# Zero rows up to 128 for every matmul that contracts over 40 or 16 rows, in a graph layer with a mixture of experts

## The chip, the cores and the metric

The kernel runs on one core of a Trainium2 chip. Its time is the device time of one execution in microseconds (us); a kernel's time is the median of its runs. TensorE is called PE below, its weight loads PEld, VectorE DVE, ScalarE ACT, GpSimd POOL, and the engine that issues most loads SP.

## The reference

There are 10000 tokens and 10000 items of width 128. A dense 10000 x 10000 adjacency matrix (400 MB in float32) is multiplied with a projection of the items; a layer of 8 experts, weighted by the two largest gate probabilities, follows.

```python
def gnn(user_feat, item_feat, adj, W_item, b_item, W_user, b_user):
    h = item_feat @ W_item.T + b_item
    b = user_feat @ W_user.T + b_user
    return relu(adj @ h + b)

def ffn(x, gate_w, gate_b, W1, b1, W2, b2):        # D = 128, H = 256, E = 8
    probs = softmax(x @ gate_w + gate_b)
    top2_vals, top2_idx = top_k(probs, 2)
    cw = zeros(N, E).at[arange(N)[:, None], top2_idx].add(top2_vals)
    for e in range(8):
        y = gelu(x @ W1[e] + b1[e], approximate=False) @ W2[e] + b2[e]
        out += cw[:, e:e+1] * y
    return out

x = x + gnn(layernorm(x), item_feat, adj, ...)
return x + ffn(layernorm(x), ...)
```

## The kernel before

**Precision.** Most products are made of three matmuls of type fp32r: an operand is split into a rounded part (hi, written by ACT) and what is left (lo, subtracted by DVE), and hi*hi, hi*lo and lo*hi are added up in PSUM. Some smaller products are plain fp32; the profile shows one of those as two records.

**The h stage** comes first. It computes h = item_feat @ W_item.T + b_item for 78 full tiles of 128 items, three tiles to a group (26 groups, four PSUM banks in turn), and for a last tile of 16 items (KREM). A group is three fp32 products (L709) and one matmul that adds the bias (L714): its weights are columns of pick_sb, its moving operand is cw_parts, whose row 0 holds the bias' hi part and row 32 its lo part. ACT copies each bank into h_hi (L358) and DVE subtracts into h_lo (L510).

**The passes.** The tokens are cut into 20 blocks of 500. Pass i (0 to 19) streams block i of the adjacency matrix in 40 steps p: 39 with two item tiles of 128 rows (one load of 500 KB each) and one, the last, with 16 rows. In each step ACT writes a_hi (L376), DVE writes a_lo (L526), and PE does three matmuls of 500 columns for each tile (L753, L754, L755) into acc. There are 5 landing buffers (raw) and 4 pairs of split buffers, so ACT and DVE can be up to four steps ahead of PE. After step 38 a dense fp32 product (L771) is added to acc.

**The work between steps.** Between the steps of pass i PE does the rest for the blocks before, at places written out by hand (STARTS, DOWN and the T_, A_, V_ numbers). For each expert e of a block: six matmuls up (L826 to L828), one "spread" (L836), which multiplies pick_sb (weights) with cw_parts and so lays the coefficients of expert e on all 128 rows of bank ps_w, and six or two matmuls down (L779 to L781, or L785 for the last two experts). cw_parts holds the coefficients' hi part in rows 0 to 7 and their lo part in rows 32 to 39, so the spread contracts over SEL_K = 40 rows. Ahead of the down products of expert 0, two more matmuls over 40 rows add the second bias (L846, L847); they come right behind the spread of expert 2. A full pass thus has 8 spreads and one last item tile. Pass 0 has no experts, pass 1 has the first four experts of one block, and after pass 19 a tail without adjacency work has twelve experts.

**Queues.** Each engine runs its own program in order and waits on semaphores. SP issues the adjacency, item and x loads; ACT's queue issues the loads of b_item, W_item and pick; POOL's queue issues those of the constants and of the expert weights.

Of the kernel before, what the change touches and what calls it, by code (L numbers as in the profile page):

```python
# [24 lines left out]
P = 128  # L25
N = 10000
D = 128
E = 8
H = 256
HH = H // P  # L30
T = 500
# [3 lines left out]
KT = N // P  # L35
KREM = N - KT * P
CT = 2
NC = KT // CT
# [8 lines left out]
I0 = RAW - ISLOTS  # L47
EPS = 1e-5
LO_ROW = 32
SEL_K = LO_ROW + E  # L50
GS = 9

assert NC * CT == KT and NG * GT == KT and NPAIR * 2 == NG and NPAIR % ISLOTS == 1
# [21 lines left out]
def build(nc, adj_main, adj_rem, xT, xR, itemT, item_rem, w_itemT, b_item, w_userT, b_user, gate_w,  # L75
          gate_b_rows, w1, b1, w2, b2, ident, before, pick, outT):
    fp32 = mybir.dt.float32
    fp32r = mybir.dt.float32r
# [4 lines left out]
    with ExitStack() as ctx:  # L83
        def sb(name, shape, dt=fp32):
            return ctx.enter_context(nc.sbuf_tensor(name, shape, dt))
# [8 lines left out]
        h_hi = sb("h_hi", [P, (KT + 1) * D], fp32r)  # L94
        h_lo = sb("h_lo", [P, (KT + 1) * D], fp32r)

        raw = [sb(f"raw{s}", [P, CT * T]) for s in range(RAW)]
        a_hi = [sb(f"a_hi{s}", [P, CT * T], fp32r) for s in range(SPL)]
        a_lo = [sb(f"a_lo{s}", [P, CT * T], fp32r) for s in range(SPL)]
# [9 lines left out]
        w2_hi = sb("w2_hi", [P, NSPLIT * HH * D], fp32r)  # L109
        w2_lo = sb("w2_lo", [P, NSPLIT * HH * D], fp32r)  # L110
        w2_sb = sb("w2_sb", [P, (E - NSPLIT) * HH * D])
        b2_hi = sb("b2_hi", [SEL_K, D], fp32r)
        b2_lo = sb("b2_lo", [SEL_K, D], fp32r)
        ident_sb = sb("ident_sb", [P, P])
        before_sb = sb("before_sb", [P, E * E])
        pick_sb = sb("pick_sb", [SEL_K, E * P], fp32r)
        power_sb = sb("power_sb", [TQ, Q])

        x_sb = sb("x_sb", [P, T])
# [7 lines left out]
        xr_sb = sb("xr_sb", [P, Q * D])  # L127
# [14 lines left out]
        rank_sb = sb("rank_sb", [TQ, Q * E])  # L142
        cw_sb = sb("cw_sb", [TQ, Q * E])

        cw_parts = sb("cw_parts", [SEL_K, T], fp32r)

        g_sb = [sb(f"g_sb{j}", [P, T]) for j in range(HH)]
        gs_hi = [[sb(f"gs_hi{s}_{j}", [P, T], fp32r) for j in range(HH)] for s in range(2)]
# [19 lines left out]
        const_landed = sem("const_landed")  # L168
        item_landed = [sem(f"item_landed{s}") for s in range(ISLOTS)]
        bias_hi_ready = sem("bias_hi_ready")  # L170
# [5 lines left out]
        w_ready = sem("w_ready")  # L176
# [55 lines left out]
        def val(ap):  # L232

            return ap.bitcast(fp32)
# [6 lines left out]
        b2_raw = xt_sb  # L241
        landing = [g_sb[0], g_sb[1], r_sb, x1_sb, x1_kept]

        def pieces(width):
# [5 lines left out]
                        for hi, lo, parts in ((w1_hi, w1_lo, w1_pieces), (w2_hi, w2_lo, w2_pieces))  # L250
                        for landed, at, width in parts]

        pick_parts = [(slice(at, at + E * P // 2), raw[0][at // (E * P // 2) * 64:at // (E * P // 2) * 64 + SEL_K, 0:E * P // 2])
                      for at in (0, E * P // 2)]
        consts = [(ident_sb, ident), (w_user_sb, w_userT), (b_user_sb, b_user), (gate_w_sb, gate_w),
                  (gate_b_sb, gate_b_rows), (b1_sb, b1), (w2_sb, w2[:, NSPLIT * HH * D:]),
                  (before_sb, before)]
# [3 lines left out]
        @block.sync  # L261
        def _(sp):
            def load_items(n, s):
                sp.dma_start(raw[I0 + s][:, 0:2 * GD], itemT[n]).then_inc(item_landed[s], 16)

            def load_step(i, p):
                s = p % RAW
                if isinstance(i, int) and i == 0 and p < RAW:
                    if s == 0:

                        sp.wait_ge(bias_ready, 3)
                    if s >= I0:

                        sp.wait_ge(h_product, NG + 1)
                else:

                    sp.wait_ge(lo_ready, i * NPOS + (p - RAW + 1))
                if p < NC:
                    sp.dma_start(raw[s][:, :], adj_main[i, p]).then_inc(raw_landed[s], 16)
                else:  # L280
                    sp.dma_start(raw[s][0:KREM, 0:T], adj_rem[i]).then_inc(raw_landed[s], 16)

            def load_xr(i):
                sp.dma_start(xr_sb[0:TQ, :], xR[i]).then_inc(xr_landed, 16)

            def load_x(i):
                sp.dma_start(x_sb[:, :], xT[i]).then_inc(x_landed, 16)

            for s in range(ISLOTS):
                load_items(s, s)  # L290
            with sp.Fori(1, NPAIR // ISLOTS) as r:
                for s in range(ISLOTS):

                    sp.wait_ge(h_product, r * (2 * ISLOTS) + (2 * s + 2 - 2 * ISLOTS))
                    load_items(r * ISLOTS + s, s)
            sp.wait_ge(h_product, NG - 2 * ISLOTS)
            load_items(NPAIR - 1, 0)
            sp.wait_ge(h_product, NG - 2 * ISLOTS + 2)
            sp.dma_start(raw[I0 + 1][:, 0:KREM], item_rem).then_inc(item_landed[1], 16)

            for p in range(NPOS):
                load_step(0, p)
                if p == I0 - 1:
                    load_xr(0)
                if p == RAW:
                    load_x(0)
            with sp.Fori(1, NB) as i:
                for p in range(NPOS):
                    load_step(i, p)
                    if p == 2:  # L310

                        sp.wait_ge(u_turned, i)
                        load_xr(i)
                    if p == RAW:

                        sp.wait_ge(x1_ready, i)
                        load_x(i)


        @block.gpsimd  # L320
        def _(pool):
            nc.gpsimd.memset(power_sb[:, :], -0.5).then_inc(power_ready, 1)
            for dst, src in consts:
                pool.dma_start(dst[:, :], src).then_inc(const_landed, 16)
            pool.dma_start(b2_raw[0:SEL_K, 0:D], b2).then_inc(const_landed, 16)
            for landed, at, width in w1_pieces:
                pool.dma_start(landed[:, 0:width], w1[:, at:at + width]).then_inc(const_landed, 16)
            pool.wait_ge(power_ready, 1)

            def user(i):  # L330
                pool.wait_ge(u_var, i + 1)
                nc.gpsimd.tensor_tensor(rstd_sb[0][:, :], var_sb[0][:, :], power_sb[:, :], ALU.pow).then_inc(u_rstd, 1)

            def tail(i):
                pool.wait_ge(t_var, i)
                nc.gpsimd.tensor_tensor(rstd_sb[1][:, :], var_sb[1][:, :], power_sb[:, :], ALU.pow).then_inc(t_rstd, 1)  # L336

            user(0)
            for n, (landed, at, width) in enumerate(w2_pieces):

                pool.wait_ge(w_ready, 2 + n + 1)
                pool.dma_start(landed[:, 0:width], w2[:, at:at + width]).then_inc(w2_landed[n], 16)
            with pool.Fori(1, NB) as i:
                tail(i)
                user(i)
            tail(NB)
# [3 lines left out]
        def _(act):  # L350
# [5 lines left out]
            def h_hi_part(b, at, rows, cols, product):  # L356
                act.wait_ge(h_product, product)
                nc.scalar.activation(h_hi[0:rows, at], ps_h[b][0:rows, 0:cols], ACT.Copy).then_inc(h_hi_ready, 1)  # L358
# [5 lines left out]
            for b in range(NG % 4):  # L364
                g = NG // 4 * 4 + b
                h_hi_part(b, slice(g * GD, (g + 1) * GD), P, GD, g + 1)
            h_hi_part(NG % 4, slice(KT * D, (KT + 1) * D), KREM, D, NG + 1)

            def split_hi(i, p):
# [119 lines left out]

        @block.vector  # L490
        def _(dve):
            nc.vector.memset(val(cw_parts[:, :]), 0.0).then_inc(bias_hi_ready, 1)
            dve.wait_ge(b_item_landed, 16)

# [34 lines left out]
            def weights(p):  # L529

                n, odd = divmod(p - W_SPLIT, 2)
                if p >= W_SPLIT and odd == 1 and n < len(weight_parts):
                    hi, lo, landed = weight_parts[n]
                    dve.wait_ge(w_hi_ready, n + 1)
                    nc.vector.tensor_tensor(lo, landed, val(hi), ALU.subtract).then_inc(w_ready, 1)
                if p == W_SPLIT:
                    dve.wait_ge(const_landed, N_CONST)
                    nc.vector.tensor_copy(b2_hi[:, :], b2_raw[0:SEL_K, 0:D]).then_inc(w_ready, 1)
                    dve.wait_ge(w_ready, 1)
                    nc.vector.tensor_tensor(b2_lo[:, :], b2_raw[0:SEL_K, 0:D], val(b2_hi[:, :]),  # L540
                                            ALU.subtract).then_inc(w_ready, 1)

            def moments(n, rows, stats_done, moments_done, var_done, count):
# [159 lines left out]
        def _(pe):  # L703
# [37 lines left out]
            def adj_step(i, p):  # L741
                q = p % SPL

                pe.wait_ge(lo_ready, i * NPOS + (p + 1))
                tiles = CT if p < NC else 1
                rows = P if p < NC else KREM
                for c in range(tiles):
                    k = p * CT + c
                    w_hi = h_hi[0:rows, k * D:(k + 1) * D]
                    w_lo = h_lo[0:rows, k * D:(k + 1) * D]  # L750
                    m_hi = a_hi[q][0:rows, c * T:(c + 1) * T]
                    m_lo = a_lo[q][0:rows, c * T:(c + 1) * T]
                    nc.tensor.matmul(acc[:, 0:T], w_hi, m_hi, start=(k == 0), stop=False)  # L753
                    nc.tensor.matmul(acc[:, 0:T], w_hi, m_lo, start=False, stop=False)  # L754
                    last = nc.tensor.matmul(acc[:, 0:T], w_lo, m_hi, start=False, stop=(k == KT))  # L755
                last.then_inc(adj_used, 1)
# [170 lines left out]
```

## Time and profile before

| | |
|---|---|
| time, median of 3 runs | 1799.37 us (1791.51 to 1808.54) |
| span of the profiled execution | 1812.4 us |
| PE busy | 1784.3 us, 98% |
| PE weight loads busy | 1359.1 us, 75% |
| DVE busy | 1467.6 us, 81% |
| ACT busy | 1239.2 us, 68% |
| mean granted clock of PE over the span | 0.993 |
| start of passes 0, 1, 2, 3, 19 | 66.9, 133.9, 206.6, 292.0, 1657.5 us |

Busy time counts a matmul from its start to its modelled end, and the matmuls overlap: one of 500 columns is shown as 0.39 us long where the next starts 0.22 or 0.23 us later. What a matmul costs in a row of them is therefore the distance from start to start. The profiled execution has no time of its own beside its span; the span stands 13 us above the median of the three timed runs, and 4 us above the slowest.

### The profile page before, as it was taken

What the parts mean: (1) busy time and instruction counts of PE and PEld (TensorE: products, weight loads), DVE (VectorE), ACT (ScalarE), POOL (GpSimd) and SP (SyncE); (2) the same over time, 40 slices, a digit from 0 to 9 for tenths busy, and PEclk for the clock granted to TensorE, in tenths of its full rate; (3) what the DMA queues carried; (4) which work ended last, traced back from release to release, by engine and by line L of the source; (5) the groups of instructions that cost most, each with busy time, mean ns of one, the idle gap of its engine ahead of it and who ended that gap; (6) DMA issues with size and microseconds to landing.
All of it is one profiled execution on the core that took longest, in us unless ns stands there. A gap on an engine that the chain in (4) does not pass through costs nothing.

```text
span 1812.4 us, 27006 instructions
## 1 busy us (share of the span) xinstructions
PE 1784.3 (98%) x7485; PEld 1359.1 (75%) x7485; DVE 1467.6 (81%) x2283; ACT 1239.2 (68%) x1601; POOL 69.6 (4%) x63
## 2 busy tenths in 40 slices
PE   8989999999999999999999999999999999999997
PEld 6767777777777777777777777777777777777764
DVE  2588888888888788888888888888887889888864
ACT  3567776766767677776766777767676777677753
POOL 1000000000000000000000000000000000000000
PEclk9999999999999999999999999999999999999997
DMA  4699777777777777777777777777777777777700
GB/s 143 230 321 324 244 260 230 244 237 253 236 243 245 242 251 241 240 251 243 238 255 234 257 218 253 236 246 245 246 248 239 243 243 244 248 251 232 256 21 12
DMA packets 124450, 423.32 MB, mean 234 GB/s; under 512 B 14251, under 2 KB 19898, under 8 KB 124430
## 3 DMA queue, kind: packets, MB, share of 16 engines
q1 hardware_dynamic: 120456, 415.41, 70.1%
q10 hardware_dynamic: 3126, 5.35, 0.8%
q0 software_dynamic: 848, 2.31, 0.4%
q8 instruction: 10, 0.16, 0.0%
q14 instruction: 10, 0.08, 0.0%
HBM read 417.90 MB, written 5.12 MB: 233 GB/s over the span
## 4 chain that ended last, share of the span: by engine, by line
PE 92%; DVE 3%; DMA 3%; ACT 2%; issue 1%; ACTq 0%; SPq 0%; DVEq 0%
PE acc L753 20%; PE acc L755 18%; PE acc L754 18%; PE ps_z L826 4%; PE ps_z L828 4%; PE ps_z L827 4%; PE ps_y L785 4%; PE ps_w L836 4%; PE ps_y L779 3%; PE ps_y L781 3%; PE ps_y L780 3%; DMA raw<-in_adj_main 2%; DVE a_lo L526 2%; PE ps_x L761 1%; PE acc L771 1%; PE ps_g L803 1%
## 5 line engine op out<-in xcount | busy, mean ns | idle before, releaser
L526 DVE TENSOR_TENSOR a_lo<-raw,a_hi 128x1000 fp32r<-128x1000 f32 (+1 forms) x800 | 930.7, 1184 | 156.2 <-ACT a_hi L376 151.6
L376 ACT ACTIVATE a_hi<-raw 128x1000 fp32r<-128x1000 f32 (+1 forms) x800 | 800.6, 1025 | 248.8 <-PE acc L755 218.4
L753 PE MATMUL acc<-a_hi,h_hi 128*128 128x500 f32 (+1 forms) x1580 | 654.1, 414 | 9.3 <-DVE a_lo L526 7.2
L755 PE MATMUL acc<-a_hi,h_lo 128*128 128x500 f32 (+1 forms) x1580 | 616.9, 390 | 0.0
L754 PE MATMUL acc<-a_lo,h_hi 128*128 128x500 f32 (+1 forms) x1580 | 615.2, 389 | 0.0
L753 PEld LDWEIGHTS acc<-a_hi,h_hi 128*128 128x128 f32 (+1 forms) x1580 | 298.1, 189 | 118.4 <-DVE a_lo L526 35.2
L755 PEld LDWEIGHTS acc<-a_hi,h_lo 128*128 128x128 f32 (+1 forms) x1580 | 297.6, 188 | 61.7
L754 PEld LDWEIGHTS acc<-a_lo,h_hi 128*128 128x128 f32 (+1 forms) x1580 | 298.6, 189 | 58.3 <-issue 8.3
L441 ACT ACTIVATE g_sb<-ps_z,b_sb 128x500 f32<-128x500 f32 x320 | 198.7, 672 | 113.5 <-DVE gs_lo L663 107.5
L663 DVE TENSOR_TENSOR gs_lo<-g_sb,gs_hi 128x500 fp32r<-128x500 f32 x240 | 151.9, 675 | 73.3 <-PE ps_y L781 72.6
L654 DVE TENSOR_TENSOR g_sb<-ps_w,g_sb 128x500 f32<-128x500 f32 x240 | 151.2, 672 | 8.8 <-ACT g_sb L441 7.0
L450 ACT ACTIVATE gs_hi<-g_sb 128x500 fp32r<-128x500 f32 x240 | 134.8, 613 | 3.2 <-DVE g_sb L654 3.2
L826 PE MATMUL ps_z<-xn_hi,w_hi 128*128 128x500 f32 x320 | 127.8, 399 | 6.8 <-ACT g_sb L441 6.7
L828 PE MATMUL ps_z<-xn_hi,w_lo 128*128 128x500 f32 x320 | 125.8, 393 | 0.0
L827 PE MATMUL ps_z<-xn_lo,w_hi 128*128 128x500 f32 x320 | 125.6, 392 | 0.0
L779 PE MATMUL ps_y<-gs_hi,w_hi 128*128 128x500 f32 x240 | 100.2, 418 | 1.1 <-DVE gs_lo L663 1.1
L781 PE MATMUL ps_y<-gs_hi,w_lo 128*128 128x500 f32 x240 | 94.4, 393 | 0.0
L780 PE MATMUL ps_y<-gs_lo,w_hi 128*128 128x500 f32 x240 | 94.1, 392 | 0.0
L336 POOL TENSOR_TENSOR rstd_sb<-var_sb,power_sb 125x4 f32<-125x4 f32 x20 | 37.4, 1870 | 1430.3 <-DVE var_sb L555 1430.3
L654 DVE TENSOR_TENSOR gs_sb<-ps_w,g_sb 128x500 f32<-128x500 f32 x80 | 50.6, 674 | 42.5 <-PE ps_y L785 40.3
L826 PEld LDWEIGHTS ps_z<-xn_hi,w_hi 128*128 128x128 f32 x320 | 60.5, 189 | 28.0 <-ACT g_sb L441 9.3
L836 PE MATMUL ps_w<-cw_parts,pick_sb 40*128 40x500 f32 x160 | 79.4, 496 | 0.0
(118 smaller groups left out, 1119.8 us busy)
## 6 DMA issues: line engine op xcount, KB each, us to landing
raw<-in_adj_main SPq DMA_DIRECT2D x780, 500.0 KB, 4.4
xr_sb<-in_xR SPq DMA_DIRECT2D x20, 250.0 KB
x_sb<-in_xT SPq DMA_DIRECT2D x20, 250.0 KB, 2.6
out<-r_sb ACTq DMA_DIRECT2D x20, 250.0 KB, 3.8
raw<-in_itemT SPq DMA_DIRECT2D x13, 384.0 KB, 3.1
g_sb<-in_w POOLq DMA_DIRECT2D x4, 250.0 KB, 5.1
raw<-in_adj_rem SPq DMA_DIRECT2D x20, 31.2 KB, 2.6
r_sb<-in_w POOLq DMA_DIRECT2D x2, 250.0 KB, 5.8
```

Of the source, the lines that this page charges most:

```text
L376: nc.scalar.activation(a_hi[q][0:rows, 0:cols], raw[s][0:rows, 0:cols], ACT.Copy).then_inc(hi_ready, 1)
L441: nc.scalar.activation(g_sb[j][:, :], ps_z[j][:, 0:T], ACT.Gelu, bias=b1_sb[:, e * HH + j:e * HH + j + 1]).then_inc(gelu_ready, 1)
L526: nc.vector.tensor_tensor(a_lo[q][0:rows, 0:cols], raw[s][0:rows, 0:cols], val(a_hi[q][0:rows, 0:cols]), ALU.subtract).then_inc(lo_ready, 1)
L654: nc.vector.tensor_tensor(scaled[:, :], ps_w[:, 0:T], g_sb[j][:, :], ALU.mult).then_inc(gs_ready, 1)
L663: nc.vector.tensor_tensor(gs_lo[j][:, :], g_sb[j][:, :], val(gs_hi[e % 2][j][:, :]), ALU.subtract).then_inc(gs_lo_ready, 1)
L753: nc.tensor.matmul(acc[:, 0:T], w_hi, m_hi, start=(k == 0), stop=False)
L754: nc.tensor.matmul(acc[:, 0:T], w_hi, m_lo, start=False, stop=False)
L755: last = nc.tensor.matmul(acc[:, 0:T], w_lo, m_hi, start=False, stop=(k == KT))
L779: nc.tensor.matmul(ps_y[:, 0:T], w2_hi[:, cols], gs_hi[e % 2][j][:, :], start=False, stop=False)
L826: nc.tensor.matmul(ps_z[j][:, 0:T], w1_hi[:, at:at + P], xn_hi[:, :], start=True, stop=False)
L827: nc.tensor.matmul(ps_z[j][:, 0:T], w1_hi[:, at:at + P], xn_lo[:, :], start=False, stop=False)
L828: nc.tensor.matmul(ps_z[j][:, 0:T], w1_lo[:, at:at + P], xn_hi[:, :], start=False, stop=True).then_inc(z_done, 1)
```

## The change

Every operand of a matmul that contracted over 40 or 16 rows gets all 128 rows, the added ones zero. pick, pick_sb, b2, b2_hi, b2_lo and cw_parts grow from 40 to 128 rows. The two halves of pick, which had landed in one raw buffer (partitions from 0 and from 64), now land in raw[0] and in xr_sb. The last tile of h_hi and h_lo is cleared first by two memsets on DVE, and PE multiplies all 128 rows of it with whatever the a_hi and a_lo buffers hold in rows 16 to 127. ACT gets one more wait, on a semaphore that DVE raises after its third memset. The order of the instructions on PE, SP and POOL is the same as before; DVE gets the two memsets at its very start, and ACT only the wait.

```diff
--- before.py
+++ after.py
@@ -47,7 +47,6 @@
 I0 = RAW - ISLOTS
 EPS = 1e-5
 LO_ROW = 32
-SEL_K = LO_ROW + E
 GS = 9
 
 assert NC * CT == KT and NG * GT == KT and NPAIR * 2 == NG and NPAIR % ISLOTS == 1
@@ -109,11 +108,11 @@
         w2_hi = sb("w2_hi", [P, NSPLIT * HH * D], fp32r)
         w2_lo = sb("w2_lo", [P, NSPLIT * HH * D], fp32r)
         w2_sb = sb("w2_sb", [P, (E - NSPLIT) * HH * D])
-        b2_hi = sb("b2_hi", [SEL_K, D], fp32r)
-        b2_lo = sb("b2_lo", [SEL_K, D], fp32r)
+        b2_hi = sb("b2_hi", [P, D], fp32r)
+        b2_lo = sb("b2_lo", [P, D], fp32r)
         ident_sb = sb("ident_sb", [P, P])
         before_sb = sb("before_sb", [P, E * E])
-        pick_sb = sb("pick_sb", [SEL_K, E * P], fp32r)
+        pick_sb = sb("pick_sb", [P, E * P], fp32r)
         power_sb = sb("power_sb", [TQ, Q])
 
         x_sb = sb("x_sb", [P, T])
@@ -142,7 +141,7 @@
         rank_sb = sb("rank_sb", [TQ, Q * E])
         cw_sb = sb("cw_sb", [TQ, Q * E])
 
-        cw_parts = sb("cw_parts", [SEL_K, T], fp32r)
+        cw_parts = sb("cw_parts", [P, T], fp32r)
 
         g_sb = [sb(f"g_sb{j}", [P, T]) for j in range(HH)]
         gs_hi = [[sb(f"gs_hi{s}_{j}", [P, T], fp32r) for j in range(HH)] for s in range(2)]
@@ -250,8 +249,7 @@
                         for hi, lo, parts in ((w1_hi, w1_lo, w1_pieces), (w2_hi, w2_lo, w2_pieces))
                         for landed, at, width in parts]
 
-        pick_parts = [(slice(at, at + E * P // 2), raw[0][at // (E * P // 2) * 64:at // (E * P // 2) * 64 + SEL_K, 0:E * P // 2])
-                      for at in (0, E * P // 2)]
+        pick_parts = [(slice(0, E * P // 2), raw[0][:, 0:E * P // 2]), (slice(E * P // 2, E * P), xr_sb[:, 0:E * P // 2])]
         consts = [(ident_sb, ident), (w_user_sb, w_userT), (b_user_sb, b_user), (gate_w_sb, gate_w),
                   (gate_b_sb, gate_b_rows), (b1_sb, b1), (w2_sb, w2[:, NSPLIT * HH * D:]),
                   (before_sb, before)]
@@ -322,7 +320,7 @@
             nc.gpsimd.memset(power_sb[:, :], -0.5).then_inc(power_ready, 1)
             for dst, src in consts:
                 pool.dma_start(dst[:, :], src).then_inc(const_landed, 16)
-            pool.dma_start(b2_raw[0:SEL_K, 0:D], b2).then_inc(const_landed, 16)
+            pool.dma_start(b2_raw[:, 0:D], b2).then_inc(const_landed, 16)
             for landed, at, width in w1_pieces:
                 pool.dma_start(landed[:, 0:width], w1[:, at:at + width]).then_inc(const_landed, 16)
             pool.wait_ge(power_ready, 1)
@@ -364,6 +362,7 @@
             for b in range(NG % 4):
                 g = NG // 4 * 4 + b
                 h_hi_part(b, slice(g * GD, (g + 1) * GD), P, GD, g + 1)
+            act.wait_ge(bias_hi_ready, 1)
             h_hi_part(NG % 4, slice(KT * D, (KT + 1) * D), KREM, D, NG + 1)
 
             def split_hi(i, p):
@@ -489,6 +488,8 @@
 
         @block.vector
         def _(dve):
+            nc.vector.memset(val(h_hi[:, KT * D:]), 0.0)
+            nc.vector.memset(val(h_lo[:, KT * D:]), 0.0)
             nc.vector.memset(val(cw_parts[:, :]), 0.0).then_inc(bias_hi_ready, 1)
             dve.wait_ge(b_item_landed, 16)
 
@@ -535,9 +536,9 @@
                     nc.vector.tensor_tensor(lo, landed, val(hi), ALU.subtract).then_inc(w_ready, 1)
                 if p == W_SPLIT:
                     dve.wait_ge(const_landed, N_CONST)
-                    nc.vector.tensor_copy(b2_hi[:, :], b2_raw[0:SEL_K, 0:D]).then_inc(w_ready, 1)
+                    nc.vector.tensor_copy(b2_hi[:, :], b2_raw[:, 0:D]).then_inc(w_ready, 1)
                     dve.wait_ge(w_ready, 1)
-                    nc.vector.tensor_tensor(b2_lo[:, :], b2_raw[0:SEL_K, 0:D], val(b2_hi[:, :]),
+                    nc.vector.tensor_tensor(b2_lo[:, :], b2_raw[:, 0:D], val(b2_hi[:, :]),
                                             ALU.subtract).then_inc(w_ready, 1)
 
             def moments(n, rows, stats_done, moments_done, var_done, count):
@@ -743,13 +744,12 @@
 
                 pe.wait_ge(lo_ready, i * NPOS + (p + 1))
                 tiles = CT if p < NC else 1
-                rows = P if p < NC else KREM
                 for c in range(tiles):
                     k = p * CT + c
-                    w_hi = h_hi[0:rows, k * D:(k + 1) * D]
-                    w_lo = h_lo[0:rows, k * D:(k + 1) * D]
-                    m_hi = a_hi[q][0:rows, c * T:(c + 1) * T]
-                    m_lo = a_lo[q][0:rows, c * T:(c + 1) * T]
+                    w_hi = h_hi[:, k * D:(k + 1) * D]
+                    w_lo = h_lo[:, k * D:(k + 1) * D]
+                    m_hi = a_hi[q][:, c * T:(c + 1) * T]
+                    m_lo = a_lo[q][:, c * T:(c + 1) * T]
                     nc.tensor.matmul(acc[:, 0:T], w_hi, m_hi, start=(k == 0), stop=False)
                     nc.tensor.matmul(acc[:, 0:T], w_hi, m_lo, start=False, stop=False)
                     last = nc.tensor.matmul(acc[:, 0:T], w_lo, m_hi, start=False, stop=(k == KT))
@@ -887,12 +887,12 @@
                                  L0_ffn_gate_w, L0_ffn_gate_b, L0_ffn_W1, L0_ffn_b1, L0_ffn_W2, L0_ffn_b2))
     eye = _np.eye(P, dtype=_np.float32)
     before = _np.tril(_np.ones((E, E), _np.float32), -1)
-    pick = _np.zeros((SEL_K, E, P), _np.float32)
+    pick = _np.zeros((P, E, P), _np.float32)
     for e in range(E):
         pick[e, e] = pick[LO_ROW + e, e] = 1.0
-    b2_rows = _np.zeros((SEL_K, D), _np.float32)
+    b2_rows = _np.zeros((P, D), _np.float32)
     b2_rows[0:E] = b2
-    b2_rows[LO_ROW:SEL_K] = b2
+    b2_rows[LO_ROW:LO_ROW + E] = b2
     blocks = adj.reshape(NB, T, N)
     arrays = {
 
@@ -914,7 +914,7 @@
         "b2": b2_rows,
         "ident": eye,
         "before": _np.broadcast_to(before.reshape(-1), (P, E * E)),
-        "pick": pick.reshape(SEL_K, E * P),
+        "pick": pick.reshape(P, E * P),
     }
     arrays = {f"in_{name}": _np.ascontiguousarray(a) for name, a in arrays.items()}
     nc = _bacc.Bacc("TRN2", target_bir_lowering=False, num_devices=1)
```

## Rows read from the trace of the kernel before

**Rows 1.** Busy time of the engines, granted clock and DMA share, in pass 0 and pass 2
```profile
67.00:134.00 67.00, 61.02 (x244) 45.97 (x245) 55.04 (x67) 47.38 (x53) 4.07 (x5) 1.00 0.94 337
...
206.60:292.00 85.40, 85.40 (x367) 65.56 (x366) 72.13 (x112) 60.60 (x78) 2.92 (x2) 1.00 0.75 244
```

**Rows 2.** Timeline (start, length, engine, line) around one spread, in pass 10
```profile
909.00 0.19 PEld L828 LDWEIGHTS ps_z<-xn_hi,w_lo 128*128 128x128 f32 x1
909.22 0.39 PE L828 MATMUL ps_z<-xn_hi,w_lo 128*128 128x500 f32 x1
...
909.54 0.49 PE L836 MATMUL ps_w<-cw_parts,pick_sb 40*128 40x500 f32 x1
...
909.97 0.49 PE L753 MATMUL acc<-a_hi,h_hi 128*128 128x500 f32 x1
...
910.30 0.39 PE L754 MATMUL acc<-a_lo,h_hi 128*128 128x500 f32 x1
...
910.52 0.39 PE L755 MATMUL acc<-a_hi,h_lo 128*128 128x500 f32 x1
```

**Rows 3.** Waits of the whole span (total, times, longest)
```profile
PEld ps_w L836 <- issue: 57.6, 159, 0.6
```

**Rows 4.** PE's timeline where down products give way to adjacency products
```profile
896.38 0.39 PE L781 MATMUL ps_y<-gs_hi,w_lo 128*128 128x500 f32 x1
896.61 0.39 PE L753 MATMUL acc<-a_hi,h_hi 128*128 128x500 f32 x1
```

**Rows 5.** PE's timeline at the last item tile of pass 9
```profile
885.06 0.49 PE L753 MATMUL acc<-a_hi,h_hi 16*128 16x500 f32 x1
...
885.94 0.49 PE L826 MATMUL ps_z<-xn_hi,w_hi 128*128 128x500 f32 x1
```

**Rows 6.** Waits inside pass 4 (377 to 462.7 us)
```profile
ACT a_hi L376 <- PE acc L755: 12.0, 13, 2.0
```

**Rows 7.** Timeline of pass 10, where the split stands closest ahead of PE
```profile
915.90 2.30 DVE L526 TENSOR_TENSOR a_lo<-raw,a_hi 128x1000 fp32r<-128x1000 f32 x2
...
918.09 0.48 PE L753 MATMUL acc<-a_hi,h_hi 128*128 128x500 f32 x1
```

**Rows 8.** Timeline of the h stage: DVE's first copy, two groups, ACT's loop head
```profile
7.12 0.48 DVE L505 CAST pick_sb<-raw 40x512 fp32r<-40x512 f32 x1 [3.97 <-DMA raw<-in_pick]
...
9.84 0.69 PE L714 MATMUL ps_v<-cw_parts,pick_sb 40*128 40x384 f32 x1
...
10.46 1.65 PE L709 MATMUL ps_g<-w_item_sb,raw 128*128 128x128 f32 x6
...
12.04 0.69 PE L714 MATMUL ps_g<-cw_parts,pick_sb 40*128 40x384 f32 x1
...
17.22 1.28 ACT L358 ACT_TABLE_LOAD   x1 [1.69 <-PE ps_x L714]
18.52 0.49 ACT L358 ACTIVATE h_hi<-ps_x 128x384 f32 x1
```

**Rows 9.** PE's timeline around a spread in the tail, granted clock 0.50
```profile
1783.60 0.62 PE L828 MATMUL ps_z<-xn_hi,w_lo 128*128 128x500 f32 x1
1784.15 0.78 PE L836 MATMUL ps_w<-cw_parts,pick_sb 40*128 40x500 f32 x1
1784.86 0.78 PE L779 MATMUL ps_y<-gs_hi,w_hi 128*128 128x500 f32 x1
1785.44 0.62 PE L780 MATMUL ps_y<-gs_lo,w_hi 128*128 128x500 f32 x1
```

**Rows 10.** PE's timeline early in pass 0
```profile
70.27 0.79 PE L753 MATMUL acc<-a_hi,h_hi 128*128 128x500 f32 x1 [0.53 <-DVE a_lo L526]
...
73.35 0.58 PE L754 MATMUL acc<-a_lo,h_hi 128*128 128x500 f32 x1
...
74.00 0.38 PE L753 MATMUL acc<-a_hi,h_hi 128*128 128x500 f32 x1
```

**Rows 11.** Waits inside pass 0 (67 to 134 us)
```profile
ACT a_hi L376 <- DMA raw<-in_adj_main: 19.1, 27, 2.4
```

## The prediction

> **What bounds the kernel now.** I read first the windows by pass, then the timeline of PE inside one, then the waits.
>
> From pass 2 on PE is the bound: it is busy for all 85.40 us of the pass while DVE has 72.13 us of work, ACT 60.60 and the DMA engines 0.75 of their time [rows 1]. Pass 0 is another matter: PE 61.02 of 67.00 us, DMA 0.94 busy [rows 1], and ACT waits 19.1 us there for adjacency data [rows 11]. So what PE saves in pass 0 and in the first part of pass 1 buys nothing; what it saves in passes 2 to 19 (18 passes) counts in full if nobody else is late.
>
> Inside a pass the matmuls of 500 columns follow each other every 0.225 us, also where one product gives way to another with other tiles, as in 896.38 to 896.61 [rows 4]. They don't around a spread [rows 2]: the 40-row matmul starts 0.32 us after the one before it, the next one 0.43 us after it, and the one behind that 0.33 us later. From 909.22 to 910.30 that is 1.08 us for three matmuls that would take 0.675: one visit to 40 rows costs **0.40 us** beyond its work. PE waits for no semaphore there; the list of waits puts it down to "issue", 57.6 us over 159 spreads, 0.36 us each [rows 3], so all of them look alike. The last item tile, with other tiles and 16 rows, does the same: 0.88 us from its first matmul to the first of 128 rows behind it, for three pitches of 0.225 [rows 5], 0.20 too much, before what comes ahead of it and just behind. The row count is what the two have in common.
>
> The Trainium skill has a rule for this and one against it. "TensorEngine Tiling (Array Packing)", Key Properties, says that a change of tiling mode drains the engine; rows 2 show such a break at both borders. "TensorE: Matmul & The Clock Gate", LDWEIGHTS, says that a weight load takes the same time whatever the number of rows, since it goes by columns, and its table on kernels adds that a single matmul over 32 rows takes as long as one over 128. Here a load takes 0.19 us at 128 rows [rows 2], so the two pages don't contradict each other: by the second alone nothing is gained or lost inside the matmul, by the first the borders go.
>
> **The change, part by part.**
>
> *Spreads and second bias in passes 2 to 19.* Eight spreads a pass; the two matmuls of the second bias stand directly behind the spread of expert 2 and share its visit. With the last item tile that is nine visits. The widened matmul itself has 500 columns as before and should take the common 0.225 us. 18 x 9 x 0.40 = **64.8 us**. Bounds for one visit: 0 if the break has another cause, 0.40 if the matmul is like any other.
>
> *Who would be late instead.* A pass becomes 85.40 - 3.6 = 81.8 us for PE; DVE's 72.13 and ACT's 60.60 still fit. Locally: the split stands closest ahead of PE where DVE ends the first of two a_lo at about 917.1 and PE takes it at 918.09 [rows 7], 1.0 us of room. Ahead of it ACT and DVE had been waiting for PE themselves (ACT 12.0 us in 13 waits in a pass, for PE to free split buffers [rows 6]). They start again when PE does, so they are pulled forward with it, and between such a wait and this place stands one visit at most, 0.40 us. That leaves 0.6 us. I take nothing off. The adjacency data must come in 81.8 instead of 85.4 us, a DMA share of 0.78 against the 0.94 that pass 0 reaches [rows 1].
>
> *Passes 0 and 1.* The visit in pass 0 is lost in the wait for data. In pass 1 I count the visits behind its last close wait, of experts 2 and 3 and the last tile: 3 x 0.40 = **1.2 us**.
>
> *The h stage.* Here PE is busy without a break too: one group from 9.84 to 12.04, 2.20 us [rows 8]. The page's line of granted clock has 9 tenths in every slice of this stage, but the durations speak against it: at 73.35 us the pitch of 500 columns falls from 0.42 to 0.23 [rows 10], and 0.42 is the pitch at a granted clock of 0.50, 1.2 GHz [rows 9]. I therefore read the h stage as run at 1.2 GHz. What a visit costs at that level rows 9 show: 0.55, 0.71 and 0.58 us where 0.42 is common, together 0.13 + 0.29 + 0.16 = 0.58. A group without it takes 2.20 - 0.58 = 1.62 us. 26 x 0.58 = **15.1 us**, and it counts in full, since the adjacency loads into four of five buffers wait for the last product of h. ACT (0.49 us a group and 1.28 us for a table load every four groups [rows 8]) and DVE have room at 1.62 us.
>
> *The clock in the h stage.* From 70.27 on PE's matmuls stand back to back at 0.42 us, and after 73.35 the clock is at its upper level [rows 10]; in the h stage before, a break comes in every 2.20 us and the clock stays down for all of it. After the change nothing breaks the groups' row. If the clock rises early in the stage, some 20 of the 26 groups run at 2.4 GHz. PE would need 0.81 us for one; ACT needs (1.28 + 4 x 0.49) / 4 = 0.81 and something for its waits, an estimate of 0.92. 20 x (1.62 - 0.92) = **14 us**. Ends: 0 if the clock stays, 26 x 0.8 = 21 if it is up from the start.
>
> *The tail* holds 12 visits. PE waits there for ACT and DVE between experts for part of the time, so a visit is worth between 0 and 0.58 us, together 0 to 7. I take **4 us**.
>
> *What the change adds.* pick grows from two loads of 80 KB (40 x 512 x 4 bytes) to two of 256 KB, beside the first item loads. DVE had waited 3.97 us for the first of them, until 7.12, and PE's first bias matmul waits for DVE [rows 8]. The 352 KB more are worth 1.1 us at pass 0's 337 GB/s [rows 1], up to 3 us if the queues share unevenly: **-1.3 us**. Two memsets of 128 columns and wider copies on DVE fall before that landing. ACT's new wait is on a memset of the first microseconds and stands in front of the last copy of h: free. b2's 64 KB for 20 are needed only in pass 0.
>
> **Sum:** 64.8 + 1.2 + 15.1 + 14 + 4 - 1.3 = 97.8 us. 1812.4 - 97.8 = 1714.6, a factor of 0.946; on the median, 1799.4 x 0.946 = **1702 us**.
>
> **The rivals.**
>
> *The clock stays down in the h stage.* The rows tell only what fp32r work of 500 columns does to the clock, not fp32 work of 128. Without the 14 us: 83.8 off, factor 0.9538, **1716 us**. Chance 0.27.
>
> *DVE or ACT takes over in part of the pass.* For it: the room of only 1.0 us at one place [rows 7]. Against it: they wait for PE 12.0 us in a pass [rows 6]. If half of the 64.8 is lost: 65 off, **1735 us**. Chance 0.08.
>
> *The break isn't the row count*, but something in these operands (pick_sb and cw_parts, or the accumulation in ps_w). Against it stands the last item tile, with h_hi and a_hi [rows 5]. Then only the later pick costs: **1800 us**. Chance 0.04.
>
> *Slower: the wider weights can no longer be loaded ahead.* The mechanism: if a load could run beside a matmul only into rows that the matmul leaves free, each of 8 spreads, 3 tile and 2 bias matmuls in 20 blocks, and 27 in the h stage, would show its 0.19 us: 20 x 13 + 27 = 287 loads, 54 us. With the breaks still there for another reason that is 1799 + 54 = **1853 us**; it decides from the point where less than two thirds of the 80 us of breaks (64.8 + 15.1) come back. Against it: the load of L828 at 909.00, 128 rows, runs while the matmul ahead of it does, and L828 still starts at the common pitch [rows 2].
> "TensorE: Matmul & The Clock Gate", "What overlaps and what doesn't", states just this rule, that loads overlap with matmuls in flight only in other row groups; these rows speak against it for full loads. Chance 0.03.
>
> **How the numbers follow.** Forecast as above 0.56, clock down 0.27, partly lost 0.08, no gain 0.04, slower 0.03; 0.02 for what I don't see. Each value stands about 8 us either way, as the three runs do. The range runs from 1688 (the clock up from the start and the tail's 7 us) to 1730 (clock down, tail worth nothing, pick 3 us late, and a slow run); the cases outside it hold less than 0.2. What a measurement can't tell from no change is 1%, 18 us: faster by more 0.94, same 0.03, slower by more 0.03.
>
> **What would show it.** In the profile after: L836 with 128 rows starts 0.225 us behind L828 and L753 or L779 0.225 behind it, "issue" before the spreads gone; passes of 81.8 us from pass 2 on, DVE at 88% of them; pass 0 starting at 38 us if the clock rose in the h stage, at 53 if it didn't; its pitch in L709 tells which. I am wrong if the pitch around the spread stays, if PE shows waits for a_lo inside passes 2 to 19, or if pass 0 and 1 grow.

## The result and the profile after

| | before | after |
|---|---|---|
| median | 1803.95 us (4 runs, 1791.51 to 1813.04) | 1713.18 us (4 runs, 1712.75 to 1714.30) |
| ratio after / before | | 0.954, 95% interval 0.950 to 0.958 |
| span of the profiled execution | 1812.4 us | 1711.2 us (its own time 1713.0) |
| PE / DVE / ACT busy, share of the span | 98% / 81% / 68% | 98% / 86% / 72% |
| first adjacency matmul (pass 0 starts) | 66.9 us | 38.6 us |
| pass 0, pass 1, each later pass | 67.0, 72.7, 85.35 us | 67.2, 71.7, 81.69 us |
| from the last adjacency matmul to the end | 73.9 us | 67.3 us |

The median before has one run more than the 1799.37 us of the prediction (1813.04). The two profiled executions differ by 101 us, the medians by 91. Where the 101 us are: 28.3 before pass 0, 1.0 in pass 1, 65.7 in passes 2 to 19 up to the last tile's first matmul, 6.5 behind it, and pass 0 is 0.3 longer. (In three executions of the kernel before pass 0 takes 65.5 to 67.0 us, so 0.3 is within what it varies. The last two figures are cut at the first matmul of the last tile, which after is recorded early, as told below; cut at its last matmul they are 65.3 and 6.9.)

The windows of the kernel after, by stage (length; busy us of PE, PEld, DVE, ACT and POOL with their counts; granted clock; DMA share; GB/s): the h stage, pass 0, pass 1, pass 2, the tail.

```profile
0.00:38.50 38.50, 27.64 (x185) 25.95 (x185) 17.19 (x35) 20.33 (x34) 7.87 (x19) 1.00 0.68 222
38.60:105.80 67.20, 61.04 (x243) 45.43 (x244) 55.12 (x67) 47.37 (x53) 4.06 (x5) 0.95 0.96 340
105.80:177.50 71.70, 69.86 (x305) 55.86 (x306) 62.20 (x95) 52.52 (x62) 3.98 (x2) 0.98 0.84 295
177.50:259.20 81.70, 81.70 (x366) 66.51 (x365) 72.11 (x112) 60.65 (x79) 2.93 (x2) 1.00 0.79 255
1643.90:1711.00 67.10, 52.42 (x200) 35.28 (x198) 37.69 (x77) 32.38 (x53) 1.01 (x1) 0.97 0.02 8
```

The same two end pieces of the kernel before:

```profile
0.00:66.90 66.90, 58.29 (x185) 43.40 (x186) 18.45 (x33) 21.64 (x34) 7.96 (x19) 1.00 0.38 121
1738.60:1812.40 73.80, 61.06 (x198) 38.18 (x198) 37.70 (x77) 32.51 (x53) 1.01 (x1) 0.85 0.02 8
```

Pass 2 answers to its row in [rows 1]: PE is still busy for all of it, and DVE's work is the same 72.11 us in a shorter pass. In pass 0 the DMA share is 0.96 and nothing was won. In the tail the granted clock is 0.97 instead of 0.85, which the prediction had not thought of.

The timeline of PE around one spread in pass 10, the place of [rows 2]:

```profile
871.24 0.38 PE L828 MATMUL ps_z<-xn_hi,w_lo 128*128 128x500 f32 x1
871.46 0.39 PE L836 MATMUL ps_w<-cw_parts,pick_sb 128*128 128x500 f32 x1
871.68 0.39 PE L753 MATMUL acc<-a_hi,h_hi 128*128 128x500 f32 x1
871.91 0.39 PE L754 MATMUL acc<-a_lo,h_hi 128*128 128x500 f32 x1
```

From L828 to L754 are 0.22 + 0.22 + 0.23 = 0.67 us, where [rows 2] have 1.08. The last item tile of pass 9, the place of [rows 5]. Its first matmul (L753, left out) is recorded from inside the fp32 product ahead, L771, so the stretch is measured from L771 on:

```profile
826.55 1.00 PE L771 MATMUL acc<-xn_sb,w_user_sb 128*128 128x500 f32 x2
...
827.63 0.39 PE L754 MATMUL acc<-a_lo,h_hi 128*128 128x500 f32 x1
827.85 0.39 PE L755 MATMUL acc<-a_hi,h_lo 128*128 128x500 f32 x1
828.08 0.39 PE L826 MATMUL ps_z<-xn_hi,w_hi 128*128 128x500 f32 x1
828.30 0.39 PE L827 MATMUL ps_z<-xn_lo,w_hi 128*128 128x500 f32 x1
```

The pitches are 0.22 and 0.23 us, so there is no break on the way out. From L771 to L827 are 1.75 us; before, the same stretch took 2.14 (884.13 to 886.27), 0.39 more, which is one visit. The h stage, which answers to [rows 8]; first the start, with DVE's first copy of pick:

```profile
8.60 0.51 DVE L506 CAST pick_sb<-raw 128x512 fp32r<-128x512 f32 x1 [5.47 <-DMA raw<-in_pick]
...
9.16 0.69 PE L715 MATMUL ps_x<-cw_parts,pick_sb 128*128 128x384 f32 x1 [2.12 <-DVE pick_sb L506]
...
10.79 0.67 PE L715 MATMUL ps_v<-cw_parts,pick_sb 128*128 128x384 f32 x1
...
12.39 0.67 PE L715 MATMUL ps_g<-cw_parts,pick_sb 128*128 128x384 f32 x1
```

Then a little later, PE and ACT's table load:

```profile
15.64 0.83 PE L710 MATMUL ps_v<-w_item_sb,raw 128*128 128x128 f32 x6
...
16.49 0.83 PE L710 MATMUL ps_g<-w_item_sb,raw 128*128 128x128 f32 x6
...
18.46 0.94 PE L710 MATMUL ps_x<-w_item_sb,raw 128*128 128x128 f32 x6
...
19.69 1.28 ACT L356 ACT_TABLE_LOAD   x1 [0.73 <-PE ps_x L715]
...
22.24 0.94 PE L710 MATMUL ps_x<-w_item_sb,raw 128*128 128x128 f32 x6
```

From 9.16 to 12.39 a group takes 1.60 to 1.63 us, as predicted for the lower clock without breaks (1.62). From 15.64 to 16.49 it takes 0.85 us: half, so the clock is up. From 18.46 to 22.24 four groups take 3.78 us, 0.945 each. One in four of them takes 1.24 instead of 0.85: PE waits at 18.46 for a bank that DVE has read by 18.41, behind ACT, whose table load comes once in four groups.

The split's distance ahead of PE, for [rows 7]. The closest place is now step 35 of pass 10:

```profile
897.19 1.19 DVE L527 TENSOR_TENSOR a_lo<-raw,a_hi 128x1000 fp32r<-128x1000 f32 x1
...
899.00 0.39 PE L753 MATMUL acc<-a_hi,h_hi 128*128 128x500 f32 x1
```

DVE ends this a_lo at 898.38, PE takes it at 899.00: 0.6 us of room. It is another place than that of [rows 7]: step 35 had 1.03 us before, and the place of [rows 7], step 14, keeps its 1.0 us (DVE ends at 857.90, PE takes it at 858.90). From pass 2 to the end of pass 19 PE waits for no a_lo. And ACT's wait for PE in a pass, for [rows 6]:

```profile
ACT a_hi L375 <- PE acc L755: 10.3, 13, 2.0
```

### The profile page after: what moved, and what is told of

It is laid out like the page before. It is cut to its first block, busy times and chain, and to the rows that moved or that the text cites. A ratio compares the mean times of both kernels' runs of the same rounds, so it can differ in the third digit from the quotient of the medians.

```text
span 1711.2 us, 27009 instructions
## 1 busy us (share of the span) xinstructions
PE 1677.4 (98%) x7485; PEld 1356.6 (79%) x7485; DVE 1466.2 (86%) x2285; ACT 1239.5 (72%) x1601; POOL 69.6 (4%) x63
## 4 chain that ended last, share of the span: by engine, by line
PE 91%; DVE 4%; DMA 3%; ACT 2%; issue 1%; ACTq 0%; DVEq 0%; SPq 0%
PE acc L753 20%; PE acc L755 20%; PE acc L754 19%; PE ps_z L826 4%; PE ps_z L827 4%; PE ps_z L828 4%; PE ps_y L785 4%; PE ps_y L779 3%; PE ps_y L781 3%; PE ps_y L780 3%; DMA raw<-in_adj_main 2%; PE ps_w L836 2%; DVE a_lo L527 2%; PE acc L771 1%; PE ps_x L761 1%; PE ps_g L803 1%
## 5 line engine op out<-in xcount | busy, mean ns | idle before, releaser
L753 PE MATMUL acc<-a_hi,h_hi 128*128 128x500 f32 x1580 | 648.0, 410 | 10.7 <-DVE a_lo L527 7.0
L755 PE MATMUL acc<-a_hi,h_lo 128*128 128x500 f32 x1580 | 617.5, 391 | 0.0
L754 PE MATMUL acc<-a_lo,h_hi 128*128 128x500 f32 x1580 | 615.2, 389 | 0.0
L753 PEld LDWEIGHTS acc<-a_hi,h_hi 128*128 128x128 f32 x1580 | 298.9, 189 | 87.2 <-issue 19.2
L754 PEld LDWEIGHTS acc<-a_lo,h_hi 128*128 128x128 f32 x1580 | 298.8, 189 | 66.3 <-issue 12.8
L755 PEld LDWEIGHTS acc<-a_hi,h_lo 128*128 128x128 f32 x1580 | 297.8, 188 | 60.7
L827 PE MATMUL ps_z<-xn_lo,w_hi 128*128 128x500 f32 x320 | 124.8, 390 | 0.0
L828 PE MATMUL ps_z<-xn_hi,w_lo 128*128 128x500 f32 x320 | 123.9, 387 | 0.0
L779 PE MATMUL ps_y<-gs_hi,w_hi 128*128 128x500 f32 x240 | 94.8, 395 | 1.1 <-DVE gs_lo L664 1.1
L785 PE MATMUL ps_y<-gs_sb,w_sb 128*128 128x500 f32 x160 | 73.9, 584 | 1.2 <-DVE gs_sb L655 1.2
```

The costliest lines, as they stand in the source:

```text
L779: nc.tensor.matmul(ps_y[:, 0:T], w2_hi[:, cols], gs_hi[e % 2][j][:, :], start=False, stop=False)
L827: nc.tensor.matmul(ps_z[j][:, 0:T], w1_hi[:, at:at + P], xn_lo[:, :], start=False, stop=False)
L828: nc.tensor.matmul(ps_z[j][:, 0:T], w1_lo[:, at:at + P], xn_hi[:, :], start=False, stop=True).then_inc(z_done, 1)
```

## The experiments

They are of two kinds: what a break hangs on, and why the kernel before spreads over more than 20 us while the kernel after spreads over 2 (1791.51 to 1813.04 against 1712.75 to 1714.30). All use the loads and buffers of the kernel after except where it says otherwise. For those with four runs or more the medians have meaning; for the others I read the length of a pass, which is the same to 0.01 us in every full pass of an execution.

### 72 rows

```diff
-  matmul(ps_w[:, 0:T], pick_sb[:, ...], cw_parts[:, :], ...)
+  matmul(ps_w[:, 0:T], pick_sb[0:72, ...], cw_parts[0:72, :], ...)
   (the same in both bias products; last item tile rows = 72)
```

> The kernel after, but every matmul that was widened contracts over 72 rows instead of 128 (same loads, same buffers). If a break comes from the border between matmuls of up to 64 rows and matmuls of more, nothing changes: 1713 us, pitch around the spread 0.225 us. If a matmul must fill all 128 rows to run without a break, the breaks are back: 1795 to 1813 us, 1.08 us for three matmuls around a spread.

Measured: 1714.60 us (1711.97 to 1716.44), full passes of 81.75 us. The timeline of PE around a spread (all lines of this kernel stand one lower than in the kernel after):

```profile
869.63 0.39 PE L829 MATMUL ps_z<-xn_hi,w_lo 128*128 128x500 f32 x1
869.85 0.39 PE L837 MATMUL ps_w<-cw_parts,pick_sb 72*128 72x500 f32 x1
870.08 0.38 PE L754 MATMUL acc<-a_hi,h_hi 128*128 128x500 f32 x1
870.30 0.39 PE L755 MATMUL acc<-a_lo,h_hi 128*128 128x500 f32 x1
```

There is no break at 72 rows. Filling the array is not what matters.

### 64 rows

The same edit with 64.

> The same with 64 rows. If the border lies at 64 rows: all breaks are back, 0.40 us a visit, 1795 to 1813 us. If the cost goes by how many rows are left empty, 64 rows are cheaper than 40: visits of 0.25 us or less, below 1770 us.

Measured: 1792.68 us (10 runs, 1786.38 to 1805.76), ratio 1.000 (0.997 to 1.004) to the kernel before on the same chip, whose median there was 1793.43. Full passes take 85.34 us. Around a spread:

```profile
871.68 0.39 PE L829 MATMUL ps_z<-xn_hi,w_lo 128*128 128x500 f32 x1
872.00 0.49 PE L837 MATMUL ps_w<-cw_parts,pick_sb 64*128 64x500 f32 x1
872.42 0.49 PE L780 MATMUL ps_y<-gs_hi,w_hi 128*128 128x500 f32 x1
872.75 0.39 PE L781 MATMUL ps_y<-gs_lo,w_hi 128*128 128x500 f32 x1
```

These are 0.32, 0.42 and 0.33 us, the three pitches of [rows 2] within 0.01. Eight more rows take all of it away: the border lies above 64 and not above 72, and below it the number of rows makes no difference between 40 and 64.

### The last tile alone

The spreads and both bias products back at 40 rows, the last tile at 128.

> The loads and buffers of after, only the last item tile keeps 128 rows. If each visit is worth the same 0.40 us whatever its tiles: passes of 85.35 - 0.40 = 84.95 us. If the spread's operands were the cause: 85.35 us. The time itself depends on the clock in the h stage, between 1780 and 1805 us.

Measured: full passes of 84.95 us. The one run took 1808.4 us, above the stated 1780 to 1805: every group of its h stage takes 2.19 us, and pass 0 starts at 68.7 us. The visit without pick_sb, cw_parts and ps_w is worth the same 0.40 us, so these operands are not the cause.

### Every spread twice

Made from the kernel before: the spread's matmul is written twice, the first without the semaphore.

> The kernel before with every spread done twice in a row (the second overwrites the first with the same values). If a break is paid per visit, a second 40-row matmul costs only its 0.225 us: passes of 85.35 + 8 x 0.225 = 87.15 us. If it is paid per 40-row matmul: 85.35 + 8 x 0.62 = 90.3 us.

Measured: full passes of 87.19 us, 1.84 us longer, 0.23 for each of the eight added matmuls. The timeline of PE around one pair:

```profile
885.22 0.39 PE L828 MATMUL ps_z<-xn_hi,w_lo 128*128 128x500 f32 x1
885.54 0.49 PE L836 MATMUL ps_w<-cw_parts,pick_sb 40*128 40x500 f32 x1
885.88 0.39 PE L838 MATMUL ps_w<-cw_parts,pick_sb 40*128 40x500 f32 x1
886.20 0.49 PE L779 MATMUL ps_y<-gs_hi,w_hi 128*128 128x500 f32 x1
886.53 0.38 PE L780 MATMUL ps_y<-gs_lo,w_hi 128*128 128x500 f32 x1
```

From L828 to the second matmul of 128 rows are 1.31 us, for four matmuls whose common pitch would make 0.90: 0.41 too much, as for one spread. What is paid is the visit, not the matmul.

### The h stage's bias alone back at 40 rows

```diff
-  matmul(ps_h[b][:, 0:tiles * D], pick_sb[:, 0:P], cw_parts[:, 0:tiles * D], ...)
+  matmul(ps_h[b][:, 0:tiles * D], pick_sb[0:40, 0:P], cw_parts[0:40, 0:tiles * D], ...)
```

> The kernel after, with only the bias matmul of the h stage back at 40 rows. If the breaks in the h stage also kept the clock down, the stage is back at 2.20 us a group at 1.2 GHz and pass 0 starts near 67 us: 1713 + 28 = 1741 us. If the clock rose in the h stage for another reason (its place in time, the other loads), the breaks cost 0.40 us a group on the upper clock: 1713 + 8 to 11 = 1722 us, pass 0 near 48 us.

Measured: 1725.21 us, and the four runs are 1720.79, 1722.87, 1727.56 and 1742.00. In the profiled one (1727.56) pass 0 starts at 54.1 us. Its timeline of PE (bias matmuls L715 only; each closes a group):

```profile
27.44 0.69 PE L715 MATMUL ps_x<-cw_parts,pick_sb 40*128 40x384 f32 x1
...
29.64 0.69 PE L715 MATMUL ps_v<-cw_parts,pick_sb 40*128 40x384 f32 x1
...
33.06 0.44 PE L715 MATMUL ps_w<-cw_parts,pick_sb 40*128 40x384 f32 x1
...
34.30 0.44 PE L715 MATMUL ps_x<-cw_parts,pick_sb 40*128 40x384 f32 x1
```

The groups take 2.20 us up to about 31 us and 1.24 us behind it: the clock rose in the middle of the stage, with the breaks in place. Neither of the two cases stated had foreseen that. A break costs 1.24 - 0.85 = 0.39 us at the upper clock and about 0.6 at the lower (2.20 - 1.62), and the rest hangs on when the clock rises. The highest run, 1742, is where a stage spent wholly on the lower clock would end (1713 + 28); that run was not profiled, so this is an inference.

### The h stage's bias alone at 128 rows

The complement: spreads, second bias and last tile back at 40 and 16 rows.

> The loads and buffers of after, but only the bias matmul of the h stage keeps 128 rows; spreads, second bias and last tile are back at 40 and 16. If the breaks are local and the clock of the h stage hangs on the stage's own breaks: pass 0 starts at 38 to 39 us in every run, passes of 85.35 us, 1713 + 18 x 3.66 + about 6 = 1785 us, and runs that agree within 2 us or so, unlike those of before. If something else made the clock rise, pass 0 starts later and the runs spread over 20 us.

Measured: 1781.40 us (1779.07 to 1782.14), ratio 0.987 (0.980 to 0.993). Windows of its h stage and tail:

```profile
0.00:39.20 39.20, 26.55 (x185) 24.86 (x185) 17.11 (x35) 20.34 (x34) 7.87 (x19) 0.99 0.72 216
...
1712.60:1780.00 67.40, 54.61 (x198) 33.31 (x198) 37.68 (x77) 32.41 (x53) 1.01 (x1) 1.00 0.02 8
```

Pass 0 starts at 39.2 us in the one profiled run, the passes are back at 85.35 us, and the four runs lie within 3 us where those of the kernel before on the same chip went from 1787 to 1812.

All profiles together say the same. In the seven whose h stage has breaks (the kernel before three times, 64 rows, the last tile alone, the spread twice, the h stage's bias at 40) the clock rose at 27.1 to 31.8 us four times and only behind the stage, at 73.2 to 74.5 us, three times. In the five without (after, 72 rows, this one, and the two with the small load of pick below) it rose at 9.8 to 15.2 us. The pair of 64 and 72 rows tells breaks from row count: with nearly as many rows in use the clock rose at 27.1 us where the breaks are and at 14.1 us where they aren't. The stage's own breaks make its clock late, and with it most of the spread of the kernel before.

### Two more executions of the kernel before

> The kernel before once more, to see why its runs spread over 21 us and those of after over 1.5. If the clock's state in the h stage differs from one execution to the next, pass 0 starts early (40 to 60 us) in a run under 1800 us and near 67 us in a run near 1812, while passes 2 to 19 keep 85.35 us. If it is the tail's clock, pass 0 starts at 67 us in any run and the part after the last adjacency matmul varies around 74 us. If neither, passes 0 and 1 (adjacency data) vary.

> The kernel before once more. Two profiles of it so far had the whole h stage on the lower clock and 1809 to 1814 us. A run below 1795 us should show the clock up before the stage's end and pass 0 at 52 us or earlier; passes of 85.35 us whatever the time.

The first of these took 1810.39 us with pass 0 at 66.3 us, the second 1795.84 us with pass 0 at 51.4 us; full passes of 85.35 us in both. The second one's timeline of PE (bias matmuls L714), and its windows (h stage, tail):

```profile
25.73 0.69 PE L714 MATMUL ps_x<-cw_parts,pick_sb 40*128 40x384 f32 x1
...
27.92 0.44 PE L714 MATMUL ps_v<-cw_parts,pick_sb 40*128 40x384 f32 x1
...
29.16 0.43 PE L714 MATMUL ps_g<-cw_parts,pick_sb 40*128 40x384 f32 x1
...
30.39 0.44 PE L714 MATMUL ps_w<-cw_parts,pick_sb 40*128 40x384 f32 x1
```

```profile
0.00:51.30 51.30, 42.23 (x185) 31.59 (x185) 18.17 (x33) 21.31 (x34) 7.95 (x19) 1.00 0.51 157
...
1722.30:1794.00 71.70, 58.83 (x198) 37.00 (x198) 37.67 (x77) 32.50 (x53) 1.01 (x1) 0.89 0.02 8
```

Groups take 2.20 us before 28 us and 1.23 us behind. With the one profiled at first that makes three executions of the same kernel: spans of 1812.4, 1808.6 and 1794.0 us, with pass 0 at 66.9, 66.3 and 51.4 us. Of the 18.4 us between the first and the last, 15.5 lie before pass 0, 0.8 in passes 0 and 1 and 2.1 in the tail. The lowest runs, 1787 us, weren't profiled; that the clock rose still earlier in them is a guess.

### A smaller load of pick, and adjacency loads issued earlier

Here DVE clears pick_sb and pick is loaded and copied with its 40 rows only, all matmuls stay at 128:

```diff
+  nc.vector.memset(val(pick_sb[:, :]), 0.0).then_inc(pick_clear, 1)
-  nc.vector.tensor_copy(pick_sb[:, cols], landed)
+  nc.vector.tensor_copy(pick_sb[0:SEL_K, cols], landed)
```

> The kernel after, but pick is loaded with its 40 rows as before and DVE clears pick_sb first. Group 0's bias matmul starts at 7.7 instead of 9.16 us, pass 0 that much earlier: 1713 - 1.5 = 1711.5 us. If the next limit in the h stage (ACT) takes it back, 1713 us.

Measured: 1710.21 us (1707.28 to 1711.91), pass 0 at 34.9 us. Bias matmuls of the first groups (L721 here), and the window of pass 0:

```profile
6.81 0.67 PE L721 MATMUL ps_x<-cw_parts,pick_sb 128*128 128x384 f32 x1
...
8.41 0.67 PE L721 MATMUL ps_v<-cw_parts,pick_sb 128*128 128x384 f32 x1
...
10.00 0.42 PE L721 MATMUL ps_g<-cw_parts,pick_sb 128*128 128x384 f32 x1
...
10.84 0.42 PE L721 MATMUL ps_w<-cw_parts,pick_sb 128*128 128x384 f32 x1
```

```profile
34.90:103.20 68.30, 60.52 (x243) 46.07 (x243) 54.64 (x67) 47.38 (x53) 4.06 (x5) 0.95 0.95 331
```

The first bias matmul starts at 6.81 instead of 9.16 us, the clock is up before 10.84 (a group of 0.84 us) instead of about 15, and pass 0 starts 3.7 us earlier. Pass 0, bound by its data (DMA share 0.95), takes 68.4 instead of 67.2 us and gives back 1.2. The tail of this execution is 1.7 us longer, at a granted clock of 0.95 instead of 0.97, so that of the 3.7 us only 1.1 show between the two profiled spans (1711.2 and 1710.1).

The last one adds to this that the first adjacency loads are issued as buffers come free (steps 3, 4, 1, 2).

> The kernel with the small pick load, and the first adjacency loads issued as each landing buffer comes free (steps 3 and 4 after 22 and 24 products of h, then 1 and 2) instead of all after the 27th. Pass 0 is bound by its data, so 1 MB that lands some 3 us earlier should shorten the way to pass 1 by up to 3 us: 1709 to 1711 us. If the loads of steps 3 and 4 push back those of 1 and 2, which PE needs first, nothing: 1711.5 us. Slower than 1713 us if ACT, which waits for step 1 first, then stalls for longer.

Measured: 1711.58 us (6 runs, 1710.33 to 1712.56), pass 0 at 35.1 us and pass 1 at 103.1 (103.3 without it). The earlier loads buy 0.2 us up to pass 1, nothing in the time. The kernel with the small load alone has the lowest median, 3.0 us or 0.2% under the kernel after. The ranges of their four runs each don't overlap, but they ran on different chips, so how much of the 3.0 us is the change stays open.

## Why the prediction was right, and where it was off

The sum against the profiled execution was 97.8 us and came out as 101.2, and the mechanism is the one named. By its parts:

- **The visit.** 0.40 us in nine visits a pass; measured 85.35 - 81.69 = 3.66 us, 0.41 a visit. The rule of the Trainium skill on mode switches ("TensorEngine Tiling (Array Packing)", Key Properties), taken there as the likely reason, agrees with the runs: by its list ("Available Configurations") the row modes end at 64, and the step lies between 64 and 72 rows. That the lost time is a drain is the page's word; the runs show only where the step lies. The page gives no price; 0.40 us at the upper clock is the runs'.
- **Who would be late.** Nobody was, as forecast, but the 0.6 us of room agree by luck in part. They were forecast for the place of [rows 7], which kept its 1.0 us; the 0.6 are at step 35, where 1.03 had been and which the prediction didn't name. That a place can lose one visit of room, 0.40 us, was right.
- **Passes 0 and 1.** 1.2 us forecast, 1.0 in pass 1 less 0.3 in pass 0. "If pass 0 and 1 grow" was named as a sign of being wrong; pass 0 did by 0.3 us, less than it varies from one execution of the kernel before to the next.
- **The h stage.** 15.1 for the breaks, 14 for the clock, 1.3 back for the load of pick: 27.8 forecast, 28.3 measured. The group came to 1.62 and 0.945 us where 1.62 and 0.92 were forecast. The load of pick cost more than its term: without it the stage is 3.7 us shorter, not 1.3. Of these 2.35 are the later first bias matmul (9.16 against 6.81 us), and the other 1.35 go with the later rise of the clock (15.2 against 10.0 us). That PE's wait for pick puts off this rise is not shown: where the first bias matmul came latest without breaks, at 10.92 us, the clock rose at 14.7.
- **The tail.** 4 us forecast, 6.5 measured, and here the reason was mostly another. The experiment with breaks in the tail but the clock up for all of it (bias alone at 128) has a tail of 67.8 us at 1.00, the kernel after one of 67.3 us at 0.97, the kernel before 73.9 us at 0.85 and, in the execution of 1794.0 us, 71.8 us at 0.89. So the length goes mostly with the clock. An estimate of what the widened matmuls are worth at the same clock: the spread-twice kernel has 72.0 us at 0.95, of which 12 x 0.225 = 2.7 are its added matmuls, and the kernel with the small load has 69.0 at 0.95, which leaves 0.3 us for twelve visits (0.6 by the other cut), and more if part of the 2.7 hides in waits of PE. Whether the change is what keeps the clock up there can't be told for certain: in seven profiles with breaks in the tail it is 0.85 to 0.90 five times, 0.95 once and 0.99 once, in five without 0.95 to 0.97.

**The step that was mis-sized** is the last one of the sum: "a factor of 0.946; on the median ... 1702 us". It took the 13 us between the profiled execution and the median as spread evenly over the kernel. They sat mostly in one term. The profiled execution had its whole h stage on the lower clock; others of the same kernel rise at 28 us and start pass 0 at 51.4, and for those the change is worth 12.8 us before pass 0, not 28.3. The kernel after doesn't share the spread, so 1714.6, the sum against the profiled span, was the number to give (1716 with the 2 us around the span); 1713.2 was measured. (The lower end of the stated range, 1688, comes to 1692 from the terms that it names.) The prediction even had the two facts side by side, a clock that was down for the whole stage and a profile above all three runs.

**The rivals.** That the clock stays down in the h stage was put at 1716 us, nearer to the result than the forecast, and is refuted all the same: from 15.64 us on a group takes 0.85 us. DVE or ACT taking over: ACT still waits 10.3 us for PE in a pass, and PE waits for no a_lo in passes 2 to 19. Another cause than rows: refuted by the last tile alone and by 64 against 72 rows. Loads that can't run ahead, the slower case: every pitch around a widened matmul is 0.22 or 0.23 us, so no load shows.

## What to carry to other kernels

Look at the distances from start to start around small matmuls in a row of large ones: here a matmul over 40 rows, with 0.225 us of work, cost 0.40 more at its borders, under no semaphore's name, and zero rows up to 72 removed it. Where small ones must stay, put them side by side, since the visit is what costs. When a profiled execution lies off the median, find the stage that varies before scaling a sum to the median; a change that removes the cause of the variation takes the best and the worst run to the same place.

## What the runs showed of the hardware that wasn't expected

- A matmul over 40, 16 or 64 rows between matmuls over 128 costs 0.40 to 0.41 us at a granted clock of 1.00; at 0.50 one over 40 rows costs 0.58 [rows 9]. Over 72 rows it costs nothing. Matmuls over 125 rows (the transposes) don't show it: from the last one to the second adjacency matmul behind are 0.34 us, for pitches of 0.11 and 0.225.
- The same program on the same inputs had its clock rise at about 28 us in one execution and only behind the h stage, at 73 us, in another, 15.5 us apart at the start of pass 0. In seven profiles with breaks in the stage it never rose between 32 and 73 us. What decides it in a stage with breaks stays open. Without the breaks it rose by 16 us in each of five profiles.
- The profile's granted clock shows the upper level ahead of its first recorded change, while the pitches there are those of the lower: 1.00 for the h stage of the kernel before, whose groups take 2.20 us as at 0.50.
